# DMA transposes in place of TensorE's for the softmax weights and the normalised rows

## The reference

```python
def _autocorrelation(Q, K, V):            # 8 heads, L = 512
    corr = ifft(fft(q) * conj(fft(k))).real
    w, idx = top_k(corr, int(2 * log(L)))  # 12 lags for each channel
    w = softmax(w)
    for i in range(topk):
        g = minimum(idx[..., i] + pos, L - 1)
        out = out + w[..., i] * take_along_axis(v, g)
x = x + _autocorrelation(layernorm(x), ctx, ctx)
h = layernorm(x)
x = x + h @ kernel + bias + (low-rank adapters, one gated sum per sequence, one shared)
```

## Time and profile before

| | |
|---|---|
| median of 3 runs | 3232.16 us (3230.66 to 3232.26) |
| the profiled execution | 3233.24 us, its span 3231.4 us |
| TensorE busy | 3107.0 us, 96% of the span |
| DVE, POOL, ACT busy | 2068.1, 1688.9, 1116.5 us |
| attention stage | to about 1667 us |
| second stage | from about 1667 us to the end |

### The profile page before, as it was taken

One profiled execution on the slowest core, in us unless ns is written; L12 is line 12 of the kernel. 1 busy time (PEld: TensorE's weight loads), 2 busy tenths in 40 slices (PEclk: granted clock), 3 DMA queues, 4 the chain that ended last, 5 costly groups with the idle time before them and its releaser, 6 DMA issues. The chain is left out here.

```text
span 3231.4 us, 39054 instructions
## 1 busy us (share of the span) xinstructions
PE 3107.0 (96%) x14899; PEld 1702.5 (53%) x14899; DVE 2068.1 (64%) x2799; ACT 1116.5 (35%) x1760; POOL 1688.9 (52%) x759
## 2 busy tenths in 40 slices
PE   5999999999999999999948999999999999999999
PEld 3566566566565665665524444444444444444444
DVE  5899999999889998999943343343344344334312
ACT  4666565666566665555311010110111011011100
POOL 6888898898888988988622122122112112212210
PEclk8999999999999999999969999999999999999999
DMA  6334434434344454343257223232222323322110
GB/s 227 122 117 151 160 116 160 145 132 163 134 156 160 143 170 145 113 150 115 71 169 264 103 84 111 87 106 101 105 91 90 117 75 111 108 104 89 66 53 27
DMA packets 145621, 396.74 MB, mean 123 GB/s; under 512 B 12272, under 2 KB 28784, under 8 KB 129904
## 3 DMA queue, kind: packets, MB, share of 16 engines
q1 hardware_dynamic: 145456, 394.43, 35.2%
HBM read 308.15 MB, written 86.25 MB: 122 GB/s over the span
## 5 line engine op out<-in xcount | busy, mean ns | idle before, releaser
L1313 PE MATMUL ps<-w_hi,h_hi 128*128 128x512 f16 x2048 | 777.4, 380 | 4.1 <-DVE xt L1425 4.1
L1314 PE MATMUL ps<-w_lo,h_hi 128*128 128x512 f16 x2048 | 776.8, 379 | 0.0
L1315 PE MATMUL ps<-w_hi,h_lo 128*128 128x512 f16 x2048 | 776.7, 379 | 0.0
L1199 POOL TENSOR_TENSOR xt<-xt,vl 128x2048 f32<-128x2048 f32 x32 | 144.1, 4505 | 998.8 <-DMA xt<-x_scratch 732.5
L809 PE MATMUL ps<-op,it 128*128 128x512 f32 x1024 | 447.5, 595 | 12.8 <-DVE op L955 12.8
L734 PE MATMUL ps<-wt,fp 128*128 128x512 f16 x1536 | 338.5, 380 | 1.4 <-DVE wt L922 1.4
L1315 PEld LDWEIGHTS ps<-w_hi,h_lo 128*128 128x128 f16 x2048 | 200.5, 98 | 242.3 <-issue 1.0
L1313 PEld LDWEIGHTS ps<-w_hi,h_hi 128*128 128x128 f16 x2048 | 200.7, 98 | 240.4 <-issue 8.0
L809 PEld LDWEIGHTS ps<-op,it 128*128 128x128 f32 x1024 | 195.3, 191 | 247.5 <-issue 230.8
L1314 PEld LDWEIGHTS ps<-w_lo,h_hi 128*128 128x128 f16 x2048 | 200.5, 98 | 227.7 <-issue 0.6
L1425 DVE SCALAR_TENSOR_TENSOR xt<-ps,w_back,xt 128x512 f32<-128x512 f32 x128 | 95.9, 749 | 350.9 <-PE ps L1315 349.8
(11 more groups left out here) (176 smaller groups left out, 5836.2 us busy)
## 6 DMA issues: line engine op xcount, KB each, us to landing
sg<-lora_ab SPq DMA_DIRECT2D x112, 512.0 KB, 4.3
cg<-ctx SPq DMA_DIRECT2D x32, 1024.0 KB, 5.2
xv<-x SPq DMA_DIRECT2D x32, 1024.0 KB, 5.3
x_scratch<-xv SPq DMA_DIRECT2D x32, 1024.0 KB, 6.2
xt<-x_scratch SPq DMA_DIRECT2D x32, 1024.0 KB, 5.0
out<-xt SPq DMA_DIRECT2D x32, 1024.0 KB, 3.9
xg<-x SPq DMA_DIRECT2D x30, 1024.0 KB, 8.4
xrow<-x SPq DMA_DIRECT2D x24, 1024.0 KB, 6.0
```

What stands on the lines that cost most here:

```text
L1199: nc.gpsimd.tensor_tensor(xt[:, k, :], xt[:, k, :], vl[:, :], ALU.add).then_inc(vl_ok, 1)
L1313: nc.tensor.matmul(ps[:, c, :], h_hi[:, k, i, :], w_hi[:, i, cols], start=(i == 0), stop=False)
L1314: nc.tensor.matmul(ps[:, c, :], h_hi[:, k, i, :], w_lo[:, i, cols], start=False, stop=False)
L1315: last = nc.tensor.matmul(ps[:, c, :], h_lo[:, k, i, :], w_hi[:, i, cols], start=False, stop=(i == KT - 1))
```

## The change

In both stages the fp16 pair is made ahead of the transposition and in SBUF, and DMA transposes, issued from ACT's queue, bring the two parts into place. TensorE's transposes go. In the attention stage the pair is `w16`, which lies in the memory of `mi`; one transpose moves two 128-channel blocks of one part (128x1024 fp16, 256 KB), so there are four for each piece. `w_rest` moves from the start of DVE's step to behind `top_lags`, ahead of `add_output`. In the second stage the normalised row is taken in two halves of 1024 columns through one buffer `h16`; the rests overwrite `h`; four transposes of 128x1024 for each tile. ACT's loops over b are written out.

```diff
-            wt = sb("wt", [P, 2, 4, GC], FP16, st)
+            wt = sb("wt", [P, 2, CT, 4, P], FP16, st)
+            w16 = [mi[:, 2 * k:2 * k + 2, :].rearrange("p a c -> p (a c)").bitcast(FP16).rearrange("p (j c) -> p j c", c=L) for k in range(2)]
@@ ACT, attention stage
+                    def weights_turned(a, k):
+                        act.dma_start_transpose(wt[:, a, 2 * k:2 * k + 2, :, :].rearrange("p j l c -> p (j l) c"),
+                                                w16[a][:, 2 * k:2 * k + 2, :].rearrange("p j l -> p (j l)")).then_inc(s_wt[a][k], 16)
                     def transposed_out(b, g):
                         n = GPB * b + g
+                        for j in range(CT):
+                            act.wait_ge(w_ready, 4 * n + j + 1)
+                            nc.scalar.activation(w16[0][:, j, :], wd[:, j, :], ACT.Copy, scale=WSCALE).then_inc(wt_hi, 1)
                         if later(b, g):
                             act.wait_ge(w_spec, 8 * n)
-                        for k in range(4):
-                            act.wait_ge(wt_spec, 4 * n + k + 1)
-                            nc.scalar.activation(wt[:, 0, k, :], ps[:, k, :], ACT.Copy, scale=WSCALE).then_inc(wt_hi, 1)
+                        for k in range(2):
+                            act.wait_ge(wt_hi, 4 * n + 2 * k + 2)
+                            weights_turned(0, k)
+                        for k in range(2):
+                            act.wait_ge(wt_lo, 4 * n + 2 * k + 2)
+                            weights_turned(1, k)
@@ TensorE, attention stage
-                            for j in range(CT):
-                                last = nc.tensor.transpose(ps[:, k, j * P:(j + 1) * P], wd[:, j, k * P:(k + 1) * P], ident[:, :])
-                            last.then_inc(wt_spec, 1)
                     def weight_spectra(b, g, lead):
                         n = GPB * b + g
-                        pe.wait_ge(wt_lo, 4 * n + 4)
+                        pe.wait_ge(w_ready, 4 * n + 4)
+                        for a in range(2):
+                            for k in range(2):
+                                pe.wait_ge(s_wt[a][k], 16 * n + 16)
@@ DVE, attention stage
                     def w_rest(b, g):
                         n = GPB * b + g
-                        for k in range(4):
-                            dve.wait_ge(wt_hi, 4 * n + k + 1)
-                            nc.vector.scalar_tensor_tensor(out=wt[:, 1, k, :], in0=ps[:, k, :], scalar=WSCALE, in1=wt[:, 0, k, :],
+                        for j in range(CT):
+                            dve.wait_ge(wt_hi, 4 * n + j + 1)
+                            nc.vector.scalar_tensor_tensor(out=w16[1][:, j, :], in0=wd[:, j, :], scalar=WSCALE, in1=w16[0][:, j, :],
                                                            op0=ALU.mult, op1=ALU.subtract).then_inc(wt_lo, 1)
                     def step(b, g, lead, convert, first=False):
-                        w_rest(b, g)
...
                         if lead:
                             top_lags(*ahead(b, g, 1), (b, g) if convert else None, None if convert else (b, g))
+                            w_rest(*ahead(b, g, 1))
                         add_output(b, g)
@@ ACT, second stage (high_of_h; normalise waits for s_hl of the tile before)
-                        for q in range(4):
-                            act.wait_ge(ht_spec, 4 * n + q + 1)
-                            nc.scalar.activation(h_hi[:, k, 4 * q:4 * q + 4, :], ps[:, 4 + q, :].rearrange("p (c t) -> p c t", t=P),
-                                                 ACT.Copy).then_inc(hi_ok, 1)
+                        act.wait_ge(h_ok, n + 1)
+                        for q in range(2):
+                            if q or later(b, t):
+                                act.wait_ge(s_hh, 32 * n + 16 * q)
+                            nc.scalar.activation(h16[:, :], h[:, q * D // 2:(q + 1) * D // 2], ACT.Copy).then_inc(hi_ok, 1)
+                            act.wait_ge(hi_ok, 2 * n + q + 1)
+                            act.dma_start_transpose(h_hi[:, k, q * KT // 2:(q + 1) * KT // 2, :], h16[:, :]).then_inc(s_hh, 16)
+                            act.wait_ge(lo_ok, 2 * n + q + 1)
+                            act.dma_start_transpose(h_lo[:, k, q * KT // 2:(q + 1) * KT // 2, :], h_rest[q]).then_inc(s_hl[q], 16)
@@ TensorE, second stage: transposes(b, t) is gone; adapter_in waits for the DMAs
-                        pe.wait_ge(hi_ok, 4 * n + 4)
-                        pe.wait_ge(lo_ok, 4 * n + 4)
+                        pe.wait_ge(s_hh, 32 * n + 32)
+                        for q in range(2):
+                            pe.wait_ge(s_hl[q], 16 * n + 16)
@@ DVE, second stage (rest_of_h)
+                        for q in range(2):
+                            dve.wait_ge(hi_ok, 2 * n + q + 1)
+                            nc.vector.tensor_tensor(h_rest[q], h[:, q * D // 2:(q + 1) * D // 2], h16[:, :], ALU.subtract).then_inc(lo_ok, 1)
```

More of the change, by code:

```diff
@@ L702, in _ @@
                         step(0, g, True, True, True, True, False)
-                    with act.Fori(1, B // 2) as b:
+                    for b in range(1, B // 2):
                         for g in range(GPB):
@@ L736, in forward_pair, with forward_w @@
                         return last
+                    def forward_w(bank, kind, part):
+                        dst = ps[:, bank, :].rearrange("p (j c) -> p j c", c=P)
+                        for k in range(2):
+                            for i, (tab, val) in enumerate(((0, 0), (1, 0), (0, 1))):
+                                last = nc.tensor.matmul(dst, fp[:, tab, k, kind, :], wt[:, val, :, 2 * part + k, :],
+                                                        start=(k == 0 and i == 0), stop=(k == 1 and i == 2))
+                        return last
                     def c_spectrum(b, g):
@@ L761, in q_spectrum, with bound_of_w @@
                             forward_pair(4 + i, i, (qh, ql[k]), i // 2).then_inc(q_spec, 1)
-                    def transpose_w(b, g, scale):
+                    def bound_of_w():
+                        pe.wait_ge(w_ready, 4 * (NG // 2) + 4)
+                        pe.wait_ge(top_ok, 1)
+                        nc.tensor.transpose(ps[0:1, 3, 0:P], wtop[:, 0:1], ident[:, :]).then_inc(top_spec, 1)
+                        pe.wait_ge(row_max, 1)
+                        nc.tensor.matmul(ps[:, 3, P:P + 1], ones[0:1, :], wtop[0:1, 1:2], start=True, stop=True).then_inc(topall_ok, 1)
+                        pe.wait_ge(top_read, 1)
@@ L764, in transpose_w, with weight_spectra @@
+                    def weight_spectra(b, g, lead):
                         n = GPB * b + g
                         pe.wait_ge(w_ready, 4 * n + 4)
-                        if scale:
-                            pe.wait_ge(top_ok, 1)
-                            nc.tensor.transpose(ps[0:1, 3, 0:P], wtop[:, 0:1], ident[:, :]).then_inc(top_spec, 1)
-                        for k in range(4):
[L770 to L773, removed]
-                            for j in range(CT):
-                                last = nc.tensor.transpose(ps[:, k, j * P:(j + 1) * P], wd[:, j, k * P:(k + 1) * P], ident[:, :])
-                            last.then_inc(wt_spec, 1)
@@ L1024, in _ @@
                     top_lags(0, 0, None, None)
+                    w_rest(0, 0)
                     for g in range(GPB):
@@ L1060, in build @@
             h = sb("h", [P, D], FP32, st)
+            h16 = sb("h16", [P, D // 2], FP16, st)
+            h_rest = [h[:, q * D // 2:(q + 1) * D // 2].bitcast(FP16)[:, 0:D // 2] for q in range(2)]
             h_hi = sb("h_hi", [P, 2, KT, P], FP16, st)
@@ L1102, in build @@
             bias_ok = sem("bias_ok", st)
-            ht_spec = sem("ht_spec", st)
+            s_hh = sem("s_hh", st)
+            s_hl = [sem(f"s_hl{k}", st) for k in range(2)]
             hi_ok = sem("hi_ok", st)
@@ L1264, in _ @@
                         step(0, t, True)
-                    with act.Fori(1, B - 1) as b:
+                    for b in range(1, B - 1):
                         for t in range(TT):
@@ L1272, in _, with adapter_in @@
                 def _(pe):
[L1273 to L1275 removed]
+                    def adapter_in(b, t):
+                        n, k = TT * b + t, t % 2
+                        pe.wait_ge(s_hh, 32 * n + 32)
+                        for q in range(2):
+                            pe.wait_ge(s_hl[q], 16 * n + 16)
                         if later(b, t):
                             pe.wait_ge(d_ok, 4 * n)
[L1278 to L1288 removed]
                         if t == 0:
@@ L1340, in step @@
                         chunk(b, t, 1, gated)
-                        if more:
-                            transposes(*nxt)
                         chunk(b, t, 2, gated)
@@ L1346, in step @@
                             adapter_in(*nxt)
-                    transposes(0, 0)
                     bounds(0, 0, 0)
```

37 lines of the change are left out of this document (11 added, 26 removed).

## The result

The changed kernel takes 3430.11 us (3427.42 to 3433.11), the kernel before 3232.09 in the same rounds: a ratio of 1.061, interval 1.060 to 1.063. The forecast was +61 us; the measured change is +198. Direction and the place of the new wait were as forecast, the size was off by a factor of three. The time lies inside the stated range of 3215 to 3450, but above the likeliest case, which ended at 3349.

The account below looks back on a forecast made before the run. The loop tying TensorE and DVE was taken to bound the attention stage, TensorE the second. Terms +82 (first half), +25 (`convert` steps), +3 (first and last piece), -49 (second stage) gave +61 on 3233.2: 3294 us, range 3215 to 3450.

Parts of the forecast that it names:

- the likeliest case: Whole kernel: attention steps from 53.1 and 49.0 us up to 56 and 52.5, total 3249 to 3349 us.
- W: Attention stage: time from a piece's last weight to its `weight_spectra`; 7.0 us before, forecast 11.8 with the POOL wait (b < 4).
- the loop's formula: Attention step: at least W plus W-to-L933 (5.4 us) plus L933 to the next weights' end (35.9, or 35.3 in `convert`).
- deadline: Second stage: transposes must land by about 2370.5, ahead of the next `adapter_in`; 11 us or more left; missing it 0.05.
- rests begin at 0, end at 2.4, the first bank is free at 3.1: `convert` steps, counted from the last weight: W = 8.3, step 49.0 us; taken as 50.5, +25 us in all.
- an instruction of 1.27 us that took 3.08: Sign from the trace before: an SBUF-only DVE instruction like the rests, longer while POOL's L404 runs, read as waiting for POOL.
- the forecast's middle case: First half: rests wait for POOL's L413, end at 5.9 us instead of 4.0; W 11.8, step 53.1.
- I take half of it: First half: lower clock ahead of `q_spectrum` would cost 3 us a step; half taken, giving 54.5, or +5.1 a step.
- I take them as just hidden: Attention stage: a piece's four DMA transposes land within the 5.8 us that W = 11.8 leaves for two issues and a landing.
- 35.9 us from L933 to the weights' end: Attention loop: DVE's stretch from L933 to the end of the next weights, busy but for about 1.5 us.
- the DMA transposes set W: Attention-stage rival, chance 0.22: a piece's four transposes follow one another; steps of 60.3 and 57.3 us, total about 3490.
- Its d: Time for each of a piece's four successive DMA transposes: decisive from about 2.2 us, 4 used in that rival's total.

Follow-up runs that it names:

- rows_only: Attention stage of the kernel before, second stage of the changed kernel: 3188.3 us, ratio to before 0.9853 to 0.9886.
- add_first: The changed kernel with DVE's rests behind `add_output` instead of ahead of it: 3509.2 us, ratio to the kernel before 1.0828 to 1.0889.
- psum_rests: The changed kernel with softmax weights kept in PSUM, where conversions and rests read them: 3396.4 us, ratio to the kernel before 1.0488 to 1.0523.
- filled: The changed kernel with 30 idle matmuls on TensorE between the last softmax weight and `q_spectrum`: 3422.7 us, ratio to the kernel before 1.0565 to 1.0600.

## Why the prediction was off

**Right.** TensorE's removed work was worth nothing in the attention stage, because W grew. TensorE idles in one piece ahead of `q_spectrum`, released by `xv`, at a clock of 0.50 behind it. In a `convert` step the loop's formula gives 35.3 + 5.4 + 15.1 = 55.8, and the step shown is 55.8 us long (the `weight_spectra` ahead of it starts at 1591.43). The second stage fell by 61.5 from its first `adapter_in` (forecast 60), and without a deadline missed. Part of that match is luck: most tiles became 1.75 us shorter (47.26 to 45.51), not 1.91, which is 54 us in 31 tiles; the rest is mainly one slow tile of before, the second, with 53.1 us. The last transpose of a tile landed 11.4 us or more ahead of `adapter_in` in twelve tiles, but only 1.0 to 2.7 us ahead in every fourth, so the deadline was nearer than "11 us or more".

**Wrong: "rests begin at 0, end at 2.4, the first bank is free at 3.1".** This is the term that failed most: +98 us in the `convert` steps, where +25 were forecast. I had written that a hold-up by POOL could add little there (1.5 us in the sum), and had given the `convert` steps no lower clock. Measured in the step shown: rests end at 7.8, W is 15.1 against the 9.8 in the sum. Of the 5.3 us of W that were missing, about 4 are the rests and 1.35 the clock (6.55 us for `q_spectrum`); in the mean of 13 such steps it is 3.4 and 2.0. I had priced the hold-up as the end of one POOL instruction for all four rests. The runs show that end for each rest in turn: POOL has three instructions in the window, and three rests wait, each until one of them has ended. POOL is slowed too, 2.80 us instead of 2.35 where it begins before a rest has ended.

The signs were in my rows: an instruction of 1.27 us that took 3.08, and POOL without a gap through these windows. I also read that row against the wrong POOL instruction. It ran from 1321.14 to 1324.22, and L404 began only at 1323.10; ahead of L404 stood

```profile
1321.02 2.12 POOL L420 TENSOR_TENSOR xg<-xg,qh 128x1024 f16<-128x1024 f32 x1
```

which ended at 1323.14, and DVE's ended 1.1 us behind it.

**Mis-sized: first half.** 54.5 a step was forecast, 57.3 measured in the mean of 15 steps. The rests ended at 5.9 as in the forecast's middle case, but at 8.0 in every fourth step, where two of them are held up: 0.4 us a step. "I take half of it" for the clock was 1.5 us, and is 2.2. "I take them as just hidden" for the transposes was 0, and is 0.5. The fourth term is a constant read from the wrong step: 35.9 us from L933 to the weights' end holds only in every fourth step of the kernel before, in the others it is 36.9, and in the changed kernel both are the same. The difference is DVE's L896, which is itself held up by POOL in 11 of 15 steps, for instance in the step ahead of the one in the earlier trace rows:

```profile
623.47 2.92 DVE L896 SCALAR_TENSOR_TENSOR ft<-wc,gsc,ft 128x1024 f32<-128x1024 f32 x1
```

With the time from W to L933, 0.3 longer in the mean, it adds 1.0 to the step. Together 2.7 us, where 2.8 are missing. The same reading error hid how close the loop was. W + 42.3 is 49.3, the step itself: in 11 of the first half's 15 steps TensorE already waited 0.25 to 0.46 us for the weights, as at 629.79 in the earlier trace rows.

**The starts.** The first `weight_spectra` begins 8.5 us later, where 3 us were forecast for the first and the last piece together. The second stage begins 16.6 to 18.3 us later (rows_only), where 11 were forecast.

**The rival "the DMA transposes set W"** decides in add_first and in psum_rests, not in the changed kernel, where only 8.1 us of its waits lie in the steps of the first half and none in the `convert` steps but the last two. Its d was too high: an issue holds ACT's queue for 1.25 us and more, and a transpose lands 3.1 us after it at the least, but four overlap. The upper part of the stated range was put there for this rival. That 3430 lies in it is luck, since the rests and the clock brought it there. The page "VectorE: DVE Perf Modes" of the Trainium skill, The three transpose paths, prices one 128x128 block; the estimate of 42 us for a piece that the prediction worked out from it, block after block, is not borne out by these runs: all four issues and landings of a piece fit into the 13.1 us from 665.10 to 678.24.

**What stays open.** That the hold-up goes when one operand is in PSUM, or when POOL is idle, is shown; why the two engines take turns on SBUF is not. Which transfer slows the transposes, the store or the loads behind it, was not separated, and a version that keeps the changed attention stage and beats the kernel before was not found.

## What to carry to other kernels

Moving work off the busiest engine pays only where the chain that feeds that engine does not grow: in the second stage the new chain fitted behind the matmuls, and a tile became 1.75 us shorter; in the attention stage the chain was already the bound in most steps of the first half, and W grew by 8. When several chains end together, undo them in pairs: each alone gave 3, 7 and 34 us or a loss, two of them gave 126 and 140. And a DVE instruction moved from PSUM to SBUF is not the same instruction where POOL is busy: count one POOL instruction for each of them. Before a constant goes into a loop's sum, read it in several steps: here one step in four was 1 us shorter than the rest.

## What the runs showed of the hardware

- A DVE `scalar_tensor_tensor` of 128x512 with all operands in SBUF took 676 to 686 ns with POOL idle (68 of 128). Beside POOL's SBUF work it took 1.5 to 2.8 us and ended 0.54 to 0.55 us behind the end of a POOL instruction (all 60 others). With one operand in PSUM it took 678 to 692 ns beside the same work. POOL's instructions that began before such a rest had ended took 2.8 instead of 2.35 us.
- A DMA transpose of 128x1024 fp16 landed in 3.2 us (median) in the second stage, 4.0 in the changed attention stage, 6.4 beside the 1 MB store in add_first. The trace counts 270336 packets for 67.14 MB on their queue, 248 bytes each. How long the issues hold ACT's queue, min/median/max in ns:

```profile
L613 ACTq DMA_TRANSPOSE wt<-mi x128: 1247/1330/3300, 91.3 to 1858.3; - x128
```

- TensorE's granted clock fell to 0.50 behind idle times of 6.8 us in the steps of the changed kernel, and `q_spectrum` began with 4 us at that level. With idle matmuls in that time (filled) `q_spectrum` took its 5.2 us again.
